# A four-layer graph network on one core: the entrance of its last layer rebuilt around a split root product

## The reference

```python
agg  = segment_sum(x[src], edge_type * n + dst)        # 34 relations
cnt  = segment_sum(ones,   edge_type * n + dst)
mean = agg / maximum(cnt, 1)
h1   = einsum('rni,rio->no', mean, W_rel) + x @ W_root + b_rgcn
xw   = h1 @ W_gcn                                      # then a normalised neighbour sum
```

## Time and profile before

| | us |
|---|---|
| median of 3 runs | 1069.91 (1068.56 to 1072.1) |
| the profiled execution, device time | 1069.65 |
| its span, first to last instruction | 1067.8 |
| TensorE busy in the span | 1029.7 (96%) |
| VectorE, ScalarE, GpSimd busy | 767.6, 574.3, 263.5 |
| mean granted TensorE clock | 0.996 of full |

### The profile page before, as it was taken

One profiled execution on the slowest core, in us unless ns is written; L12 is line 12 of the kernel. 1 busy time (PEld: TensorE's weight loads), 2 busy tenths in 40 slices (PEclk: granted clock), 3 DMA queues, 4 the chain that ended last, 5 costly groups with the idle time before them and its releaser, 6 DMA issues.

```text
span 1067.8 us, 17748 instructions
## 1 busy us (share of the span) xinstructions
PE 1029.7 (96%) x7444; PEld 853.1 (80%) x7444; DVE 767.6 (72%) x1106; ACT 574.3 (54%) x612; POOL 263.5 (25%) x166
## 2 busy tenths in 40 slices
PE   8999999999999999999899989999999999999997
PEld 6799986454689984445869879967999999999994
DVE  7993855888754237888654495755989898989873
ACT  0433216888633338888324373424767676767650
POOL 3524704899400027988100000000000000000000
PEclk9999999999999999999999999999999999999999
DMA  8033247221042374221335302614978787878740
GB/s 302 12 126 142 90 144 233 63 66 55 6 178 89 119 231 144 60 60 41 109 129 187 125 1 90 214 49 155 302 254 281 256 279 254 280 256 279 255 168 32
DMA packets 82324, 163.20 MB, mean 153 GB/s; under 512 B 4076, under 2 KB 60168, under 8 KB 81950
## 3 DMA queue, kind: packets, MB, share of 16 engines
q1 hardware_dynamic: 80768, 151.86, 42.0%
q0 software_dynamic: 1472, 10.15, 3.4%
HBM read 158.35 MB, written 0.80 MB: 149 GB/s over the span
## 4 chain that ended last, share of the span: by engine, by line
PE 81%; DVE 11%; issue 3%; ACT 2%; DMA 1%; POOL 0%; SPq 0%; DVEq 0%; ACTq 0%
PE PS L1139 20%; PE PS L803 8%; PE PS L974 7%; PE PS L819 6%; PE PS L602 5%; PE PS L701 5%; PE PS L1122 5%; PE PS L725 4%; PE PS L532 4%; PE PS L621 3%; PE PS L545 3%; PE PS L1155 2%; PE PS L1041 2%; DVE PRD L1756 2%; PE PS L861 2%
## 5 line engine op out<-in xcount | busy, mean ns | idle before, releaser
L2025 DVE TENSOR_TENSOR Wlo<-W,Whi 128x2304 fp32r<-128x2304 f32 x68 | 172.1, 2550 | 18.9 <-ACT Whi L1496 18.9
L1496 ACT CAST Whi<-W 128x2304 fp32r<-128x2304 f32 x68 | 144.4, 2126 | 0.0
L1139 PE MATMUL PS<-Whi,Mhi 128*128 128x384 f32 x408 | 138.1, 338 | 0.0
L1139 PE MATMUL PS<-Wlo,Mhi 128*128 128x384 f32 x408 | 136.6, 335 | 0.0
L1139 PE MATMUL PS<-Whi,Mlo 128*128 128x384 f32 x408 | 136.5, 335 | 0.0
L499 POOL TENSOR_TENSOR PRDP<-arena 128x1024 f32<-128x1024 f32 x48 | 114.7, 2390 | 33.0 <-issue 20.6
L803 PE MATMUL PS<-QH,SEL 128*128 128x512 f32 x384 | 115.8, 422 | 5.9 <-DVE PRD L1756 1.5
L1338 ACT ACTIVATE arena<-PS 128x1024 f32<-128x1024 f32 x96 | 98.5, 1026 | 24.2 <-PE PS L803 24.2
L803 PEld LDWEIGHTS PS<-QH,SEL 128*128 128x128 f32 x384 | 64.8, 188 | 55.8 <-DVE PRD L1756 21.5
L1338 ACT ACTIVATE PS<-PS 128x1024 f32<-128x1024 f32 x96 | 98.0, 1021 | 2.6 <-PE PS L803 2.6
L1139 PEld LDWEIGHTS PS<-Whi,Mhi 128*128 128x128 f32 x408 | 76.9, 188 | 0.4 <-DVE Wlo L2025 0.2
(11 more groups left out here) (306 smaller groups left out, 2421.1 us busy)
## 6 DMA issues: line engine op xcount, KB each, us to landing
W<-in_L_rel SPq DMA_DIRECT2D x68, 1152.0 KB, 6.5
W<-in_W_rel SPq DMA_DIRECT2D x6, 2304.0 KB, 9.2
W<-in_W SPq DMA_DIRECT2D x6, 2304.0 KB, 9.1
arena<-in_qU SPq DMA_DIRECT2D x96, 128.0 KB, 2.7
W<-in_WqT SPq DMA_DIRECT2D x4, 2304.0 KB, 8.7
W<-in_W_root SPq DMA_DIRECT2D x2, 2304.0 KB, 13.3
W<-in_WgT SPq DMA_DIRECT2D x2, 2304.0 KB, 8.5
QH<-QH POOLq DMA_DIRECT2D x2, 1536.0 KB, 9.7
```

Of the source, the lines that this page charges most:

```text
L1139: mm = pe.matmul(PS[:, 4 + s % 2, 0:HALF], MS[a][mb][:, k, j * P:(j + 1) * P], WS[b][w % 3][:, k, :], start=n == 0, stop=n == 17)
L1496: nc.scalar.copy(WS[0][w % 3][:], W[(FIRST34 + r) % 2][:, :, q * HALF:(q + 1) * HALF]).then_inc(w_hi, 1)
L2025: V.tensor_tensor(WS[1][w % 3][:], W[(FIRST34 + r) % 2][:, :, q * HALF:(q + 1) * HALF], WS[0][w % 3][:].bitcast(F32), ALU.subtract).then_i ...
```

## The change

The edits, all at the entrance of the last layer:

1. **Root product in three passes.** The high part of the root weights (`ROOT`, two halves of 128 x 2304) and of turned `x` (`XTS[0]`) is made by ScalarE, the remainders (`ROOTL`, `XTS[1]`) by VectorE. Per tile and half, `root_half` issues 18 fp32r products of 128 x 384: six hi·hi, six hi·lo, six lo·hi. `ROOT` and `XTS` use buffers of the pair loop that are not yet in use (the third `WS`, the second `MS`); `ROOTL` lies in the rows of biases that earlier layers have used up and in `xT`.
2. **Where the splitting stands.** ScalarE splits off `ROOT` before the square root of the last normalisation; VectorE makes the remainder of half 0 (`root_lo(0)`) after the first half tile of layer 3's result, that of half 1 (`root_lo(1)`) after tile 0 is normalised.
3. **First pair.** Its one-hots are made before layer 3's results are added; `count_pair(0)` and 12 instead of 16 warm-up products stand between the two turnings; the copy to `BB` follows at once. Slots and source sums stand between the four root halves.
4. **Releases.** VectorE raises `w_used` to 23 after the last remainder of the root weights, so SP sends relation 1 from there. `weight_hi(2)` waits for `root_done`, raised by the last root half.
5. **Branch.** TensorE reads the flag and branches ahead of the root product, not behind it.

The diff, cut to its core:

```diff
-        WS = [[put(..., 41 + 18 * q + 9 * i) for q in range(3)] ...]
+        WS = [[put(..., 41 + 18 * q + 9 * i) for q in (0, 2, 1)] ...]
+        ROOT, ROOT_M, XTS = (WS[0][2], WS[1][2]), FIRST34 - 1, (MS[0][1], MS[1][1])
+        ROOTL = [nc.alloc_sbuf_tensor_at(f"ROOTL{i}", [P, n, HALF], F32R, offset=at)
+                 for i, (n, at) in enumerate(((KC, at_h + 15360), (4, at_w + (2 * KC + NT) * FEAT * 4), (2, at_h + 27648)))]
 TensorE
-            to_turned(4, xN, ready=..., between=lambda: keep_busy(16, 7)).then_inc(x_turned, 1)
-            m = FIRST34 - 1
-            weights(m)
-            natural(0, xT, W[m % 2], ready=x_ready(2)).then_inc(w_used, 1)
+            def root_half(t, h):
+                pe.wait_ge(wt_ready, 3 * 2 * R3 + h + 1)
+                for a, b in ((0, 0), (0, 1), (1, 0)):
+                    for k in range(KC):
+                        if t == h == 0 and b == 0 and k % 2 == 0:
+                            pe.wait_ge(ts_ready if a else ts_hi, 3 * 2 + k // 2 + 1)
+                        mm = pe.matmul(PS[:, 2 * t + h, 0:HALF], XTS[a][:, k, t * P:(t + 1) * P], root_low(h, k) if b else ROOT[h][:, k, :],
+                                       start=a == b == k == 0, stop=a == 1 and k == KC - 1)
+                return mm
+            def first_counts():
+                keep_busy(12, 7)
+                count_pair(0)
+            to_turned(4, xN, ready=..., between=first_counts).then_inc(x_turned, 1)
             overflow = pe.value_load(flag[0:1, 0:1])
             with pe.If(overflow < 1):
+                root_half(0, 0)
+                count_slots(0)
+                root_half(0, 1)
                 pe.wait_ge(xs_ready, 1)
-                count_pair(0)
-                count_slots(0)
-                for i in range(3):
-                    sum_sources(0, i)
+                sum_sources(0, 0)
+                root_half(1, 0)
+                sum_sources(0, 1)
+                sum_sources(0, 2)
+                root_half(1, 1).then_inc(root_done, 1)
 ScalarE
+            for h in range(2):
+                act.wait_ge(w_in[ROOT_M % 2], 16 * (ROOT_M // 2 + 1))
+                nc.scalar.copy(ROOT[h][:], W[ROOT_M % 2][:, :, h * HALF:(h + 1) * HALF]).then_inc(wt_hi, 1)
             norm_x(3)
-            turn_x(3)
+            act.wait_ge(b_done, 1)
+            nc.scalar.copy(BB[:], PS[:, 7, :]).then_inc(bb_ready, 1)
+            act.wait_ge(x_turned, 2)
+            for i in range(3):
+                nc.scalar.copy(XTS[0][:, 2 * i:2 * i + 2, :], PS[:, 4 + i, :]...).then_inc(ts_hi, 1)
 VectorE
+                    for j in range(2):
+                        pair_onehots(0, j)
                     for t in range(NT):
                         for part in range(2):
...
+                            if t == part == 0:
+                                root_lo(0)
                         then(ins)
                         normalise_tile(3, t)
+                        if t == 0:
+                            root_lo(1)
-            dve.wait_ge(x_turned, 2)
-            middle_copy(1)
+            for i in range(3):
+                dve.wait_ge(ts_hi, 3 * 2 + i + 1)
+                V.tensor_tensor(XTS[1][:, 2 * i:2 * i + 2, :], PS[:, 4 + i, :]..., XTS[0][...].bitcast(F32), ALU.subtract).then_inc(ts_ready, 1)
...
                 V.tensor_tensor(XS[1][:], xN[:], XS[0][:].bitcast(F32), ALU.subtract).then_inc(xs_ready, 1)
+                count_inverse(0)
                 weight_lo(0)
+                sums_lo(0, 0)
                 weight_lo(1)
-                count_inverse(0)
+                for i in range(1, 3):
+                    sums_lo(0, i)
                 for j in range(2):
                     pair_onehots(1, j)
-                for i in range(3):
-                    sums_lo(0, i)
```

More of the change, by code:

```diff
@@ L227, in build, with root_low @@
         SLOTB = hN[0:R34, 1, 0:128].bitcast(BF16)
-        WS = [[put(f"W{x}{q}", [P, KC, HALF], F32R, 41 + 18 * q + 9 * i) for q in range(3)] for i, x in enumerate(("hi", "lo"))]
+        WS = [[put(f"W{x}{q}", [P, KC, HALF], F32R, 41 + 18 * q + 9 * i) for q in (0, 2, 1)] for i, x in enumerate(("hi", "lo"))]
         MS = [[put(f"M{x}{b}", [P, KC, NODES], F32R, (95 if b else 0) + 6 * i) for b in range(2)] for i, x in enumerate(("hi", "lo"))]
         XS = [nc.alloc_sbuf_tensor_at(f"X{x}", [P, NT, FEAT], F32R, offset=at_h + 6144 * i) for i, x in enumerate(("hi", "lo"))]
+        turned = lambda a: a.rearrange("(t p) n -> p t n", t=KC)
+        WgT, WqT = A["WgT"], A["WqT"]
+        gate_w = [WgT[0:FEAT], WqT[0:FEAT], WqT[FEAT:]]
+        stream = [WgT[FEAT:], A["W_root1"]] + [A["W_rel1"][r] for r in range(R3)] + gate_w
+        stream += [A["W_root2"]] + [A["W_rel2"][r] for r in range(R3)] + gate_w
+        stream += [A["L1_W"]] + [A["W1"][r] for r in range(R3)] + [A["W2"][r] for r in range(R3)] + [A["L3_root"]]
+        FIRST34 = len(stream)
+        LOOP34 = (R34 - 2) // 2
+        ROOT, ROOT_M, XTS = (WS[0][2], WS[1][2]), FIRST34 - 1, (MS[0][1], MS[1][1])
+        ROOTL = [nc.alloc_sbuf_tensor_at(f"ROOTL{i}", [P, n, HALF], F32R, offset=at)
+                 for i, (n, at) in enumerate(((KC, at_h + 15360), (4, at_w + (2 * KC + NT) * FEAT * 4), (2, at_h + 27648)))]
+        def root_low(h, k):
+            return ROOTL[0][:, k, :] if h == 0 else ROOTL[1][:, k, :] if k < 4 else ROOTL[2][:, k - 4, :]
+        root_done = sem("root_done")
         BB = put("BB", [P, NT * NODES], F32R, 12)
@@ L289, in build @@
         h_turned, hN_ready = sem("h_turned"), sem("hN_ready")
[L290 removed]
+        var_ready, sd_ready, ln_done, x_turned = (sem(n) for n in ("var_ready", "sd_ready", "ln_done", "x_turned"))
         gcn_scaled, gcn_sum = sem("gcn_scaled"), sem("gcn_sum")
         cn_turned, cn_copied = sem("cn_turned"), sem("cn_copied")
[L293 removed]
+        rows_done, gcn_act, gcn_dve, evicted = (sem(n) for n in ("rows_done", "gcn_act", "gcn_dve", "evicted"))
         wl_hi, wl_ready, wl_used = sem("wl_hi"), sem("wl_ready"), sem("wl_used")
@@ L321, in build @@
             sem(n) for n in ("msum_done", "ms_hi", "ms_ready", "w_hi", "w_lo", "y_done", "y_hi", "y_ready", "scat_done", "ct_ready"))
[L324 to L331, removed]
         block = ctx.enter_context(nc.Block())
@@ L1165, in last_product @@
                 natural(0, hT, W[m % 2], ready=sums_ready(2), half_sem=rows_done).then_inc(w_used, 1)
+            def first_counts():
+                keep_busy(12, 7)
+                count_pair(0)
+            to_turned(4, xN, ready=lambda t: pe.wait_ge(ln_done, 2 * 2 + t + 1), between=first_counts).then_inc(x_turned, 1)
             overflow = pe.value_load(flag[0:1, 0:1])
             with pe.If(overflow < 1):
+                root_half(0, 0)
+                count_slots(0)
+                root_half(0, 1)
                 pe.wait_ge(xs_ready, 1)
-                count_pair(0)
-                count_slots(0)
-                for i in range(3):
-                    sum_sources(0, i)
+                sum_sources(0, 0)
[3 more added lines that the diff above has]
+                root_half(1, 1).then_inc(root_done, 1)
                 for p in range(PAIRS34):
@@ L1192, in _ @@
             with pe.Else():
+                for t, h in product(range(NT), range(2)):
+                    mm = root_half(t, h)
+                mm.then_inc(root_done, 1)
+                pe.wait_ge(bb_ready, 1)
                 pe.wait_ge(s1_ready, 1)
@@ L1372, in norm_x @@
                     nc.scalar.activation(sd[:, t:t + 1], mv[:, t, 1:2], ACT.Sqrt, bias=eps[:, 0:1]).then_inc(sd_ready, 1)
[L1374 to L1377, removed]
             def sums_out(n):
@@ L1483, in _ @@
                     turned_hi(4)
+            for h in range(2):
+                act.wait_ge(w_in[ROOT_M % 2], 16 * (ROOT_M // 2 + 1))
+                nc.scalar.copy(ROOT[h][:], W[ROOT_M % 2][:, :, h * HALF:(h + 1) * HALF]).then_inc(wt_hi, 1)
             norm_x(3)
-            turn_x(3)
+            act.wait_ge(b_done, 1)
+            nc.scalar.copy(BB[:], PS[:, 7, :]).then_inc(bb_ready, 1)
+            act.wait_ge(x_turned, 2)
+            for i in range(3):
+                nc.scalar.copy(XTS[0][:, 2 * i:2 * i + 2, :], PS[:, 4 + i, :].rearrange("p (k n) -> p k n", k=2)).then_inc(ts_hi, 1)
             def weight_hi(w):
@@ L1493, in weight_hi @@
                 act.wait_ge(rel_w_in[r % 2][q], 16 * (r // 2 + 1))
+                if w == 2:
+                    act.wait_ge(root_done, 1)
                 if w >= 3:
@@ L1527, in _ @@
                 weight_hi(1)
-                counts_hi(0)
                 for i in range(3):
@@ L1863, in gcn_out, with pair_onehots, root_lo @@
                     normalise_tile(2 * n, t)
-            def middle_copy(n):
-                V.tensor_copy(xT[:, 2:4, :], PS[:, 5, :].rearrange("p (k n) -> p k n", k=2)).then_inc(xT_dve, 1)
+            def pair_onehots(p, j):
+                if p and j == 0:
+                    dve.wait_ge(c_done, p)
+                for e in range(2):
```

(18 more changed lines are left out.)

16 lines of the change are left out of this document (4 added, 12 removed).

## The result

In the first comparison the changed kernel took 1064.4 us (median of 4 runs, 1063.75 to 1066.33) beside 1070.95 of the kernel before; the ratio is 0.9945, 95% interval 0.9921 to 0.9968. A second comparison, of five rounds, gave 1065.07 beside 1069.04, ratio 0.9962 (0.9948 to 0.9975), that is 4.1 us less, 2.7 to 5.6 with the interval. The forecast was 4.5 less, 1065.4.

The account below looks back on a forecast made before the run. TensorE, busy 96%, was taken to bound the kernel; entrance terms of 17.63 us plus 0.27 late start made 17.90 against 22.42, a gain of 4.5 from the median 1069.91: 1065.4 us, 8-in-10 range 1064.0 to 1067.3.

Parts of the forecast that it names:

- The sum: From the second turning to the first half product: 17.63 us, plus late start 0.27, against 22.42, a gain of 4.5.
- VectorE's chain: VectorE's added work before tile 1 starts the second turning 0.27 us later; rival that it comes later: 1066.7, chance 0.08.
- The estimate for the two subtractions: VectorE's `root_lo(1)`: 1.76 us for 128 x 1536 plus about 0.96 for 128 x 768, overlap 0.1.
- The table load: ScalarE's square-root table load, behind both root weight copies at 707.9 to 709.2, stays hidden with 0.8 us to spare.
- The rule of the Trainium skill: Drain of 1.38 us on each ScalarE table load, before tile 0's square root; as a rival 1066.0, chance 0.03.
- The loop: Pair loop is TensorE's at 17.75 us a pair, so what is gained before it stays.
- The gain was not given back: Rival: pair loop fed by weights, or waits of `weight_hi(2)` bind; within 0.3%, about 1069, chance 0.03.
- The branch: TensorE's branch before the root product taken at 0; rivals: shows a little, 1066.9, chance 0.07; long fetch, slower, 0.03.
- the clock: Rival: TensorE's clock falls to half level after pauses at the entrance, three us losing 1.5; 1066.9, chance 0.06.
- The transfers: Number of transfers stays; relation 1 goes 20 us earlier, at about 714, and nothing is gained or lost.
- It worked in time before, so the gain is nothing: Relation 1, held 50.1 us until the root product ended, goes 20 us earlier; that release was priced at nothing.
- The forecast for `weight_hi(2)`: Waiting for `root_done` at about 735.3, its remainder is ready at 740.1, wanted at 743.3: slack 3.2 us.

Follow-up runs that it names:

- the early copy: Changed kernel with the high part of the root weights' first half copied before ScalarE's copy of the last turned probabilities; entrance 20.3 us instead of 20.5.
- the plain fp32 product: Changed kernel's new order, but four root halves of six plain fp32 products, no splitting, relation 1 sent when they are done; 1074.01 us in one run.

## Why the prediction was right

- **The sum.** 17.63 forecast from the second turning to the first half product, 17.69 measured. That close a match is in part luck: the four root halves took 13.09 where 12.94 was forecast (the second one, behind the slots, 3.23), and the sums 2.86 where 2.96 was. The split product alone took 12.96. The terms of the sum give 2.5 for the split, late tile included, and 2.0 for the order; alone they gave 2.6 and 2.0.
- **VectorE's chain.** 0.27 late forecast, 0.19 measured, and the early copy gives back 0.2. The step was right in kind as well: computing the remainder twice starts the turning its full 2.8 later. The estimate for the two subtractions, 2.62, was met (the row says 2.62).
- **The table load.** It stood behind the two copies and was hidden. The rule of the Trainium skill on top of it (page "ScalarE: Activation LUTs", section "What ACT_TABLE_LOAD costs", a drain of 1.38 us with each switch to another table set) does not hold in this trace: the load ended at 710.94, and the square root began at 711.62, right when its input came; by an estimate from the page's figure it could not have begun before 712.3.
- **The loop.** 17.75 a pair and 296.9 in all in every kernel whose weights came in time. The gain was not given back.
- **Rivals.** The branch cost nothing that shows. In both profiles of the changed kernel the clock stayed at 1.00 over the pauses of 0.57 and 0.77. It stayed there over 1.87 too, in one profile; behind 3.36 it fell, at 1.4 us. The transfers did not bind, but only because their release had moved.
- **The step that was mis-judged**: "It worked in time before, so the gain is nothing". That weighed the earlier release against the old order. There the third half product came 12.8 us after the release (734.9 to 747.70). With the handovers moved in front of the last root half it comes 7.8 after that half ends (737.06 to 744.82), and the transfer with both splits took 10.7 (738.53 to 749.24 with the plain fp32 product) and 10.4 (735.63 to 746.01 with relation 1 sent late). Left where it was, the release would have cost 4.1 of the 4.5. The forecast for `weight_hi(2)`, its remainder ready 3.2 ahead of use, was met with 2.9 (741.87, wanted at 744.82), but only because the weights were there.
- **The absolute time.** 1065.4 was made on a median of three runs. The runs of one kernel spread by up to 3.5 us, so the ratio of the five rounds, 0.9962, is the measure: 0.9958 was forecast.

## What to carry to other kernels

When a queue is closed up, look at what was hidden in the gaps: a transfer released at the end of the old stage loses exactly the cover that the stage gave up, and here that would have eaten nine tenths of the gain. Price a change of a few us in the stretch between two events that it lies between, not in the total: the entrance of the changed kernel repeated to 0.02 us, the totals to some 3. See that the event at the end is recorded alike in both kernels: here the first record of a product misled by 0.3 in one of them. And where an engine waits for a whole of two parts, ask whether the first part has products of its own: that gave 2.8 us more than the whole change's 4.5.

## What the runs showed of the hardware

- The clock near the program's start differs from run to run with the same instructions: over 11 to 14 us TensorE had 1.00 granted in one profile and 0.50 in the other, and all that followed stood 1.5 us later. The mean granted clock from 4 to 60 us was 0.94, 0.97 or 1.00 in the twelve profiles.
- The length of a pause did not tell whether the clock fell. The same pause of 2.0 to 2.2 us before the same products, at 52 to 55 us, was followed by 0.50 in eight of the twelve profiles (the earlier trace rows is one) and by 1.00 in four. At the entrance it stayed at 1.00 after 1.87 and fell after 3.36. Two pauses close together, 1.57 and 1.41, left it alone with relation 1 sent late; 1.91 and 1.42 at the same place did not with the plain fp32 product.
- The root product took 15.72 us as 24 plain fp32 products and 12.96 as 72 of fp32r, 0.66 and 0.18 each: three passes cost TensorE 18% less, before the price of making the parts.
